# Graph layer kernel: the first six edge tiles of a phase are turned in two groups of three instead of three groups of two

## Chip, cores and metric

The kernel runs on one core of a Trainium2 chip. The metric is the device time of one execution in microseconds (us). Lower is better.

## What is computed

A normalised input goes through three graph layers and is added to the input. 10000 nodes have 512 features; 5000 edges lead from `src` to `dst`.

```
h = relu(layernorm(x))
for layer 0, 1, 2:
    p   = relu(h @ Wp.T + bp)
    agg = segment_sum(p[src], dst) / max(count(dst), 1)
    h   = agg @ Wl.T + bl + h @ Wr.T
    if layer < 2: h = layernorm(relu(h)) * g + be
out = x + h
```

## The kernel before

The three layers are three phases (`l` = 0, 1, 2). A phase has a node part and an edge part. The node part works on tiles of 128 nodes; 71 of the 79 tiles get their product with `Wr` there (`node_product`), the other 8 are "late" tiles, turned at the end of the edge part. The edge part works on 40 tiles of 125 edges, in 10 groups of 4: the normalised rows of the source nodes are gathered, turned, projected with `Wp`, summed along sorted edges, multiplied with `Wl` and added to the rows of the destination nodes.

Every product is made of three fp32r products (low with high, high with low, high with high), so that each operand exists as a high and a low part. To be an operand, a tile must be turned: four 128x128 transposes on TensorE write one PSUM bank (`turn`, L746). ScalarE copies the bank to the high part (`node_xt_high`, L933; `edge_xt_high`, L982), VectorE subtracts that from the bank to get the low part (`xt_low_of`, L1067 in phase 0, L1070 later) and counts `xt_low_done`. Turns use banks 0 and 1 alternately, through all turns of the program, and turn `c` waits until the low part of turn `c - 2` is made.

The order on each engine is written out by hand as one loop over steps `i` of the node part. Step `i` on TensorE holds the turn of node tile `i + 2`, the product of node tile `i` (L758 to L760, 12 matmuls), and whatever else is placed there; the last step with a product is 70. `edge_turns(l, i)` tells every engine which edge tiles are turned in step `i`: TensorE turns them behind the product, ScalarE and VectorE copy and subtract at the end of their step. VectorE's `node_out` of step `i` moves the sum of product `i - 1` out of PSUM. Tiles 6 and 7 are turned behind the first of four projections of group 0 (`project(l, 0, 0)`, L827 to L829, 12 matmuls each). That projection waits for the low parts of tiles 0 to 3. The third projection waits until VectorE has read the first one (`h_pre_of`, L1285). `h_pre`, a scan, `h_high` and `h_low` follow for each projection.

Edge rows are gathered by GpSimd (L610), eight slots deep: once all normalised rows are stored, gathers 0 to 7 are issued, and gather `t` from 8 on waits for the turn of tile `t - 8`. TensorE waits for a tile's gather before it turns it.

Of the kernel before, what the change touches and what calls it, by code (L numbers as in the profile page):

```python
# [25 lines left out]
GROUP = 4  # L26
# [7 lines left out]
AHEAD_XN = 5  # L34
AHEAD_TURN = 2
LATER = (10, 20)
EDGE_TURNS_AT = 3
LATE = 8
LATE_AT = 4
LATE_OUT_AT = (-8, -6, -4, -2, 0)  # L40
# [29 lines left out]
def sage_kernel(nc, x_in, src_cols, dst_cols, dst_rows, weights, out):  # L70
# [20 lines left out]
    with ExitStack() as ctx:  # L91
# [209 lines left out]
        product_count = [NODE_TILES - c for c in late_count]  # L301
# [71 lines left out]
        def is_product(l, n):  # L373
            return 0 <= n < product_count[l]
# [30 lines left out]
        def node_steps(l):  # L405
            return range(-AHEAD_RELU, product_count[l] + 1)

        def edge_turns(l, i):

            first = 2 * (i - (product_count[l] - EDGE_TURNS_AT))  # L410
            return range(first, first + 2) if 0 <= first < 2 * EDGE_TURNS_AT else []

        def edge_turns_beside(s):

# [5 lines left out]
        def late_turns(l, s):  # L420

            first = LATE_TURNS * (s - (EDGE_TILES - GROUP))
            return range(first, first + LATE_TURNS) if first >= 0 and late_count[l] else []
# [307 lines left out]
        def _(pe):  # L731
            def keep_busy(count):

                for _ in range(count):
                    nc.tensor.matmul(bank[7][:, 0:P], ones[:], ones[:], start=True, stop=True)
# [13 lines left out]
            def node_turn(l, t):  # L749
                u = unit_of[l][t]  # L750
                pe.wait_ge(n_xn, l * NODE_TILES + u + 1)
                turn(xn[:, u % XN_RING, :], node_no(l, t))
# [11 lines left out]
            def node_product(l, t):  # L764
                n = products_until(l) + t
                pe.wait_ge(xt_low_done, node_no(l, t) + 1)
                if t >= 4:
                    pe.wait_ge(n_out, n - 3)
                elif l:
                    pe.wait_ge(late_out_done, LATE * l - 3 + t)  # L770
                r_product(l, node_xt(True, t), node_xt(False, t), bank[4 + t % 4][:], n_product)
# [5 lines left out]
            def late_product(l, j):  # L777
                pe.wait_ge(xt_low_done, late_no_of(l, j) + 1)
                if j >= 4 and l == LAYERS - 1:

                    pe.wait_ge(xt_low_done, late_no_of(l, LATE - 1) + 1)
                    pe.wait_ge(e_h_pre, EDGE_TILES * LAYERS)
                elif j >= 4:
                    pe.wait_ge(late_out_done, LATE * l + j - 3)
                else:
                    pe.wait_ge(e_out, EDGE_TILES * (l + 1) - 3 + j)
                r_product(l, late_xt(True, j), late_xt(False, j), bank[late_bank(l, j)][:], late_product_done)

            def count(t):
                pe.wait_ge(hot_done, t + 1)  # L790
                nc.tensor.matmul(bank[2][:, 0:P], hot[:, t % HOT_RING, 0, :], hot[:, t % HOT_RING, 1, :],  # L791
                                 start=(t == 0), stop=(t == EDGE_TILES - 1)).then_inc(counted, 1)

            def turn_carry():
                pe.wait_ge(continues_done, 1)
                pe.wait_ge(counts_copied, 1)
                nc.tensor.transpose(bank[2][0:EDGE_TILES, 0:EDGE_ROWS], continues[0:EDGE_ROWS, :],
                                    ident[0:EDGE_ROWS, 0:EDGE_ROWS]).then_inc(carry_turned, 1)

            def shift_p(l):  # L800
                pe.wait_ge(shift_parts, parts_until(l, "p"))
                for m in range(K):
                    last = nc.tensor.matmul(bank[2][:, m:m + 1], shift_sum[:, m * P:(m + 1) * P], ones[:, 0:1],
                                            start=True, stop=True)
                last.then_inc(shift_p_product, 1)
# [6 lines left out]
            def edge_turn(l, t):  # L812
                pe.wait_ge(e_gathered[t % IN_RING], edge_dma(l, t, IN_RING))
                turn(rows_in[:, t % IN_RING, :], edge_no_of(l, t))
# [38 lines left out]
            for l in range(LAYERS):  # L853
                for i in node_steps(l):

                    if (l, i) == (0, 0):
                        node_product(l, i)
                    if is_product(l, i + AHEAD_TURN):
                        node_turn(l, i + AHEAD_TURN)
                    if (l, i) == (0, -AHEAD_TURN):  # L860
                        keep_busy(WARM_BETWEEN)
                    if l and 0 <= i + LATE < LATE:
                        late_product(l - 1, i + LATE)
                    if is_product(l, i) and (l, i) != (0, 0):
                        node_product(l, i)
                    if l == 0 and 0 <= i - STEP_COUNT < EDGE_TILES // COUNTS:
                        for q in range(COUNTS):
                            count((i - STEP_COUNT) * COUNTS + q)
                    if l == 0 and i == STEP_SORTED + 1:
                        turn_carry()  # L870
                    if l and i == STEP_SHIFT_P:
                        shift_p(l)
                    for t in edge_turns(l, i):
                        edge_turn(l, t)

                for m in range(GROUP):
                    project(l, 0, m)
                    if m == 0:
                        for t in range(2 * EDGE_TURNS_AT, 2 * GROUP):
                            edge_turn(l, t)  # L880
                for s in range(EDGE_TILES):
                    g, i = s // GROUP, s % GROUP
                    for t in edge_turns_beside(s):
                        edge_turn(l, t)
                    for j in late_turns(l, s):
                        late_turn(l, j)
                    if g + 1 < GROUPS:
                        project(l, g + 1, i)
                    edge_product(l, s)
                if l + 1 < LAYERS:  # L890
                    shift_z(l + 1)
# [4 lines left out]
        def _(act):  # L896
# [111 lines left out]
            for l in range(LAYERS):  # L1008
                for i in node_steps(l):
                    for u in units_at(l, i + AHEAD_STD):  # L1010
                        node_std(l, u)

                    if (l, i) == (0, 0):
                        for u in units_at(l, i + AHEAD_XN):
                            node_norm(l, u)
                    if is_product(l, i + AHEAD_TURN):
                        node_xt_high(l, i + AHEAD_TURN)
                    if l:
                        for u in units_at(l, i + AHEAD_RELU):
                            node_relu(l, u)  # L1020
                    if (l, i) != (0, 0):
                        for u in units_at(l, i + AHEAD_XN):
                            node_norm(l, u)
                    for k in R_CHUNKS.get(i, ()) if l == 0 else ():
                        high_r(0, k)
                    if 0 <= i - STEP_SPLIT_P < K:
                        high_p(l, i - STEP_SPLIT_P)
                    if 0 <= i - STEP_SPLIT_L < K:
                        high_l(l, i - STEP_SPLIT_L)
                    for t in edge_turns(l, i):  # L1030
                        edge_xt_high(l, t)
                    for u in units_at(l, i + AHEAD_XN):
                        store_xn(l, u)

                for t in range(2 * EDGE_TURNS_AT, 2 * GROUP):
                    edge_xt_high(l, t)
                for m in range(GROUP):
                    h_high_of(l, 0, m)
                for s in range(EDGE_TILES):
                    g, i = s // GROUP, s % GROUP  # L1040
                    if s >= 1:
                        edge_out(l, s - 1)
                    for t in edge_turns_beside(s):
                        edge_xt_high(l, t)
                    for j in late_turns(l, s):
                        late_xt_high(l, j)
                    if g + 1 < GROUPS:
                        h_high_of(l, g + 1, i)
                    if l + 1 < LAYERS and 0 <= s - STEP_SPLIT_R < K:
                        high_r(l + 1, s - STEP_SPLIT_R)  # L1050
                edge_out(l, EDGE_TILES - 1)

        @block.vector
        def _(dve):
# [248 lines left out]
            for l in range(LAYERS):  # L1303
# [44 lines left out]


                h_pre_of(l, 0, 0)  # L1350
                for t in range(2 * EDGE_TURNS_AT, 2 * GROUP):
                    edge_xt_low(l, t)
                h_sum_of(l, 0, 0)
                for m in range(1, GROUP):
# [6 lines left out]
                for s in range(EDGE_TILES):  # L1361
                    g, i = s // GROUP, s % GROUP
# [60 lines left out]
```

## Time and profile before

| | |
|---|---|
| median of 3 runs | 1511.41 us (1511.03 to 1511.58) |
| the profiled execution | 1511.98 us |
| its span, first to last instruction | 1510.2 us |
| mean granted TensorE clock | 0.999 |
| TensorE matmul busy | 1499.4 us, 99% of the span |
| VectorE busy | 969.7 us, 64% |
| ScalarE busy | 684.0 us, 45% |
| GpSimd busy | 603.7 us, 40% |

In the profile PE is TensorE's matmuls and PEld its weight loads, DVE is VectorE, ACT is ScalarE, POOL is GpSimd and SP is SyncE. A row of the timeline has the start in us, the duration in us, engine, line, operation, destination and sources, shapes, the number of merged instructions, and, in brackets, how long the engine stood idle ahead of it and what ended that. Ends of matmuls are modelled; their starts tell more.

### The profile page before, as it was taken

The numbers are of one execution on the slowest core, as the hardware profiler recorded it, in microseconds if no ns is written. First come the engines' busy times: TensorE is split into PE (matmuls) and PEld (weight loads), VectorE is DVE, ScalarE is ACT, GpSimd is POOL, SyncE is SP. The second block draws the span as 40 slices with busy tenths as digits, with TensorE's granted clock in tenths as the row PEclk, the third lists the DMA queues.
The fourth block names the chain that finished last, engine by engine and source line by source line (L and its number), as shares of the span: only waits on it lengthen the run. The fifth ranks groups of instructions, "written<-read, shape, count | busy, mean of one in ns | idle before, by whom it ended". The sixth has DMA issues, their size and how long they took to land.

```text
span 1510.2 us, 21142 instructions
## 1 busy us (share of the span) xinstructions
PE 1499.4 (99%) x7265; PEld 1224.3 (81%) x7265; DVE 969.7 (64%) x2084; ACT 684.0 (45%) x1267; POOL 603.7 (40%) x532
## 2 busy tenths in 40 slices
PE   9999999999999999999999999999999999999999
PEld 7788888888888888888888888888888877888887
DVE  7999766556555686776565555568767746555552
ACT  5546552322323676776232232357677732232221
POOL 4764355666523000100444432334464463444221
PEclk9999999999999999999999999999999999999999
DMA  9999875555544888786654555489999984554535
GB/s 325 333 358 299 278 258 175 115 91 90 92 84 58 265 272 303 265 287 237 195 112 84 93 89 91 54 255 345 385 354 371 378 257 86 91 89 86 95 58 146
DMA packets 157734, 298.14 MB, mean 197 GB/s; under 512 B 21565, under 2 KB 21756, under 8 KB 157500
## 3 DMA queue, kind: packets, MB, share of 16 engines
q1 hardware_dynamic: 93180, 169.02, 32.6%
q0 software_dynamic: 29744, 64.57, 24.8%
q10 hardware_dynamic: 34704, 63.19, 11.4%
q8 instruction: 59, 0.97, 0.3%
q14 instruction: 47, 0.39, 0.1%
HBM read 136.54 MB, written 160.08 MB: 196 GB/s over the span
## 4 chain that ended last, share of the span: by engine, by line
PE 97%; DMA 1%; issue 1%; SPq 0%; DVE 0%; POOL 0%; ACT 0%
PE bank L758 14%; PE bank L760 14%; PE bank L759 14%; PE bank L746 10%; PE bank L850 7%; PE bank L848 7%; PE bank L849 7%; PE bank L828 7%; PE bank L827 7%; PE bank L829 7%; DMA rows_in<-x 0%; DMA residual<-x 0%; DMA rows_in<-node_x,sorted_src 0%; PE bank L791 0%; PE bank L810 0%
## 5 line engine op out<-in xcount | busy, mean ns | idle before, releaser
L758 PE MATMUL bank<-w_high,h_low 128*128 128x512 f32 x876 | 365.2, 417 | 0.0
L759 PE MATMUL bank<-w_low,h_high 128*128 128x512 f32 x876 | 346.1, 395 | 0.0
L760 PE MATMUL bank<-w_high,h_high 128*128 128x512 f32 x876 | 345.3, 394 | 0.0
L992 ACT ACTIVATE h_high<-h_pre 128x500 fp32r<-128x500 f32 x120 | 74.7, 622 | 450.0 <-DVE h_pre L1294 448.0
L610 POOL DMA_INDIRECT rows_in<-node_x,sorted_src x120 | 123.2, 1027 | 249.8 <-PE bank L746 173.8
L760 PEld LDWEIGHTS bank<-w_high,h_high 128*128 128x128 f32 x876 | 165.5, 189 | 39.9
L827 PE MATMUL bank<-xt_low,w_high 128*128 128x500 f32 x480 | 195.8, 408 | 1.8 <-issue 1.8
L848 PE MATMUL bank<-w_high,h_low 128*125 128x512 f32 x480 | 190.7, 397 | 0.0
L850 PE MATMUL bank<-w_high,h_high 128*125 128x512 f32 x480 | 190.0, 396 | 0.0
L759 PEld LDWEIGHTS bank<-w_low,h_high 128*128 128x128 f32 x876 | 165.4, 189 | 29.6
L849 PE MATMUL bank<-w_low,h_high 128*125 128x512 f32 x480 | 189.3, 394 | 0.0
L758 PEld LDWEIGHTS bank<-w_high,h_low 128*128 128x128 f32 x876 | 165.0, 188 | 29.5 <-DVE h_low L1067 0.2
L637 POOL DMA_INDIRECT node_z<-rows_out,into_i x80 | 128.8, 1610 | 149.6 <-ACT rows_out L1005 118.2
L967 ACT ACTIVATE xn<-rows_in,off,rstd 128x512 f32<-128x512 f32 x237 | 188.0, 804 | 0.0
L828 PE MATMUL bank<-xt_high,w_high 128*128 128x500 f32 x480 | 187.7, 391 | 0.0
L1285 DVE TENSOR_SCALAR h_pre<-bank,bias_p 128x500 f32<-128x500 f32 x120 | 88.6, 738 | 154.2 <-PE bank L829 153.5
L829 PE MATMUL bank<-xt_high,w_low 128*128 128x500 f32 x480 | 187.1, 390 | 0.0
L1070 DVE TENSOR_TENSOR h_low<-bank,h_high 128x512 fp32r<-128x512 f32 x146 | 100.7, 691 | 132.9 <-ACT h_high L933 126.4
L933 ACT ACTIVATE h_high<-bank 128x512 fp32r<-128x512 f32 x213 | 125.5, 589 | 92.5 <-PE bank L746 81.8
L1105 DVE BATCH_NORM_STATS2 stats<-rows_in 128x6 f32<-128x512 f32 x237 | 159.9, 683 | 8.8 <-DMA rows_in<-x 8.8
L628 POOL TENSOR_TENSOR residual<-residual,bias_z 128x512 f32<-128x512 f32 x79 | 102.2, 1295 | 114.6 <-DMA residual<-x 114.5
L1294 DVE TENSOR_TENSOR_SCAN h_pre<-carry,h_pre 128x500 f32<-128x500 bf16 x120 | 143.9, 1200 | 3.8
(116 smaller groups left out, 2265.4 us busy)
## 6 DMA issues: line engine op xcount, KB each, us to landing
node_x<-xn ACTq DMA_DIRECT2D x237, 256.0 KB
rows_in<-node_z SPq DMA_DIRECT2D x158, 256.0 KB
node_z<-rows_out SPq DMA_DIRECT2D x142, 256.0 KB
out<-rows_out SPq DMA_DIRECT2D x79, 256.0 KB, 3.8
rows_in<-x SPq DMA_DIRECT2D x78, 256.0 KB
residual<-x SPq DMA_DIRECT2D x78, 256.0 KB, 5.3
rows_in<-node_x SPq DMA_DIRECT2D x24, 256.0 KB, 2.6
node_z<-bias_z SPq DMA_DIRECT2D x16, 256.0 KB
```

What stands on the lines that cost most here:

```text
L746: last = nc.tensor.transpose(bank[c % 2][:, k * P:(k + 1) * P], rows[:, k * P:(k + 1) * P], ident[:])
L758: nc.tensor.matmul(psum, low[:, k, :], w_high("r", l)[:, k, :], start=(k == 0), stop=False)
L759: nc.tensor.matmul(psum, high[:, k, :], w_low("r", l)[:, k, :], start=False, stop=False)
L760: last = nc.tensor.matmul(psum, high[:, k, :], w_high("r", l)[:, k, :], start=False, stop=(k == K - 1))
L827: nc.tensor.matmul(psum, w_high("p", l)[:, k, cols], low[:, k, :], start=(k == 0), stop=False)
L828: nc.tensor.matmul(psum, w_high("p", l)[:, k, cols], high[:, k, :], start=False, stop=False)
L829: last = nc.tensor.matmul(psum, w_low("p", l)[:, k, cols], high[:, k, :], start=False, stop=(k == K - 1))
L848: nc.tensor.matmul(psum, low, w_high("l", l)[:, m, :], start=(m == 0), stop=False)
L849: nc.tensor.matmul(psum, high, w_low("l", l)[:, m, :], start=False, stop=False)
L850: last = nc.tensor.matmul(psum, high, w_high("l", l)[:, m, :], start=False, stop=(m == K - 1))
L967: S.activation(xn[:, to, :], rows_in[:, slot, :], ACT.Identity, bias=off[:, slot:slot + 1], scale=rstd[:, slot:slot + 1]).then_inc(n_xn, 1)
L1105: V.bn_stats(stats[:, slot, :], rows_in[:, slot, :]).then_inc(n_stats, 1)
```

## The change

The six edge tiles that are turned in the node part are turned in two steps, three in each, where they were turned in three steps, two in each. Before: tiles 0 and 1 in step 68, 2 and 3 in step 69, 4 and 5 in step 70. After: tiles 0, 1 and 2 in step 69, and 3, 4 and 5 in step 70. The loops over the last two tiles of the first two groups (tiles 6 and 7) are written with the new constant and have the same bounds as before.

```
-EDGE_TURNS_AT = 3
+EDGE_TURNS_AT = 2
+EDGE_TURNS = 3
...
         def edge_turns(l, i):

-            first = 2 * (i - (product_count[l] - EDGE_TURNS_AT))
-            return range(first, first + 2) if 0 <= first < 2 * EDGE_TURNS_AT else []
+            first = EDGE_TURNS * (i - (product_count[l] - EDGE_TURNS_AT))
+            return range(first, first + EDGE_TURNS) if 0 <= first < EDGE_TURNS * EDGE_TURNS_AT else []
...
                     if m == 0:
-                        for t in range(2 * EDGE_TURNS_AT, 2 * GROUP):
+                        for t in range(EDGE_TURNS * EDGE_TURNS_AT, 2 * GROUP):
                             edge_turn(l, t)
...
-                for t in range(2 * EDGE_TURNS_AT, 2 * GROUP):
+                for t in range(EDGE_TURNS * EDGE_TURNS_AT, 2 * GROUP):
                     edge_xt_high(l, t)
...
-                for t in range(2 * EDGE_TURNS_AT, 2 * GROUP):
+                for t in range(EDGE_TURNS * EDGE_TURNS_AT, 2 * GROUP):
                     edge_xt_low(l, t)
```

## Rows read from the trace of the kernel before

**Rows 1.** The page: busy time of each engine, and the chain by engine.

```profile
PE 1499.4 (99%) x7265; PEld 1224.3 (81%) x7265; DVE 969.7 (64%) x2084; ACT 684.0 (45%) x1267; POOL 603.7 (40%) x532
...
PE 97%; DMA 1%; issue 1%; SPq 0%; DVE 0%; POOL 0%; ACT 0%
```

**Rows 2.** What TensorE waited for in the run: total us, times, longest.

```profile
PE bank L746 <- issue: 2.3, 3, 1.0
PE bank L827 <- issue: 1.8, 1, 1.8
...
PE bank L746 <- DMA rows_in<-node_x,sorted_src: 0.6, 1, 0.6
```

**Rows 3.** The timeline of phase 0, end of the node part, all engines.

```profile
235.16 0.48 PE L758 MATMUL bank<-w_high,h_low 128*128 128x512 f32 x1
...
237.34 0.40 PE L758 MATMUL bank<-w_high,h_low 128*128 128x512 f32 x1
...
238.04 1.03 PE L746 MATMUL bank<-ident,rows_in 128*128 128x128 f32 x8
...
238.82 0.95 POOL L610 DMA_INDIRECT rows_in<-node_x,sorted_src  x1 [0.30 <-issue]
...
241.39 1.07 ACT L982 ACTIVATE xt_high<-bank 128x500 fp32r<-128x500 f32 x2 [5.35 <-remote]
...
241.62 0.95 POOL L610 DMA_INDIRECT rows_in<-node_x,sorted_src  x1 [1.85 <-remote]
242.01 1.27 DVE L1067 SCALAR_TENSOR_TENSOR xt_low<-bank,xt_high 128x500 fp32r<-128x500 f32 x2 [4.65 <-issue]
...
242.84 1.21 PE L746 MATMUL bank<-ident,rows_in 128*128 128x128 f32 x8 [0.96 <-issue]
...
243.81 0.48 PE L758 MATMUL bank<-w_high,h_low 128*128 128x512 f32 x1
...
246.69 1.03 PE L746 MATMUL bank<-ident,rows_in 128*128 128x128 f32 x8
...
247.48 0.47 PE L827 MATMUL bank<-xt_low,w_high 128*128 128x500 f32 x1
```

**Rows 4.** The timeline of TensorE at the same place of phase 1.

```profile
734.86 1.03 PE L746 MATMUL bank<-ident,rows_in 128*128 128x128 f32 x8
...
739.64 1.22 PE L746 MATMUL bank<-ident,rows_in 128*128 128x128 f32 x8 [0.95 <-issue]
...
744.28 0.47 PE L827 MATMUL bank<-xt_low,w_high 128*128 128x500 f32 x1
```

**Rows 5.** Timelines of phase 2, one engine after the other.

```profile
1231.68 0.60 PE L746 MATMUL bank<-ident,rows_in 128*128 128x128 f32 x4
1232.64 0.66 PE L746 MATMUL bank<-ident,rows_in 128*128 128x128 f32 x4 [0.36 <-issue]
...
1240.77 0.66 PE L746 MATMUL bank<-ident,rows_in 128*128 128x128 f32 x4 [0.57 <-DMA rows_in<-node_x,sorted_src]
1241.18 0.47 PE L827 MATMUL bank<-xt_low,w_high 128*128 128x500 f32 x1
...
1249.62 0.49 PE L827 MATMUL bank<-xt_low,w_high 128*128 128x500 f32 x1 [1.83 <-issue]
...
1232.31 0.59 ACT L982 ACTIVATE xt_high<-bank 128x500 fp32r<-128x500 f32 x1 [2.63 <-issue]
...
1241.69 0.59 ACT L982 ACTIVATE xt_high<-bank 128x500 fp32r<-128x500 f32 x1 [0.86 <-PE bank L746]
1248.88 1.07 ACT L982 ACTIVATE xt_high<-bank 128x500 fp32r<-128x500 f32 x2 [6.60 <-remote]
...
1248.82 0.74 DVE L1285 TENSOR_SCALAR h_pre<-bank,bias_p 128x500 f32<-128x500 f32 x1 [5.24 <-PE bank L829]
...
1244.55 0.95 POOL L610 DMA_INDIRECT rows_in<-node_x,sorted_src  x1 [0.30 <-issue]
1245.80 0.94 POOL L610 DMA_INDIRECT rows_in<-node_x,sorted_src  x1 [0.30 <-issue]
```

**Rows 6.** Busy us by engine in one stretch of phase 2, granted clock, DMA share, GB/s.

```profile
1249.60:1262.00 12.40, 12.38 (x51) 9.99 (x52) 11.99 (x16) 3.79 (x7) 3.72 (x4) 0.86 0.30 81
```

## Prediction

> **What bounds the kernel now.** I read the page's busy times and its chain first. TensorE is busy for 1499.4 of 1510.2 us and 97% of the chain that ended last is TensorE [rows 1], so an edit moves the time by what it does to TensorE's order and pauses. The waits by engine come next: in the whole run TensorE waits some 7 us, of which the largest items are three pauses ahead of turns (2.3 us), one ahead of a projection (1.8 us) and one on a gather (0.6 us) [rows 2]. All three items lie at the end of the node part of a phase, where the change is made, so I read the timeline there.
>
> Phase 0 [rows 3]. The reader should follow one chain. The pair of turns of edge tiles 0 and 1 starts at 238.04. The copy of tile 0 on ScalarE starts only at 241.39, the low part on VectorE at 242.01, and the turn of tile 2, which wants the bank that tile 0 held, at 242.84. TensorE stood for 0.96 us by the row. Product 70 starts at 243.81 and the projection at 247.48. The late link is the first one: ScalarE saw the signal of a turn whose records end near 238.5 only at 241.4, and GpSimd, which waits for the same signal before the gather of tile 8, went on at 241.62. Until 239.8 GpSimd issued gathers back to back. Phase 1 repeats this: turns at 734.86 and 739.64, with 0.95 us idle [rows 4].
>
> Phase 2 differs [rows 5]. ScalarE's copy of tile 0 follows its turn (1231.68) at 1232.31, so signals are on time; tile 1's turn waited 0.36 us and tile 5's 0.57 us for its gather. The signals of the first projection and of turns 6 and 7 then come late: VectorE's h_pre starts at 1248.82 and ScalarE's copy of tile 6 at 1248.88, though the projection ran from 1241.18 to about 1244. The last gather ahead of that started at 1245.80. TensorE idles 1.83 us, and the granted clock is 0.86 in the stretch behind it [rows 6].
>
> **The change, part by part.** Nothing is added: the same 72 transposes, copies and subtractions of six tiles in each of three phases. What moves is the order: tiles 0 and 1 go from behind product 68 to behind product 69, tile 2 stays there as a third, tile 3 goes behind product 70 as the first of three. No DMA is issued by a turn; the gathers of tiles 0 to 7 do not wait for turns, those of tiles 8 to 13 wait for turns 0 to 5. They come later by at most one product and are not wanted before tile 8 is turned beside the first edge product. The edits to the loops of the last two tiles keep their bounds (six and eight) and cost nothing.
>
> The prices, from rows:
> - A pair of turns ahead of the next matmul takes 247.48 - 246.69 = 0.79 us; the eight transposes of rows 3 make 0.44 us a turn, so a last turn costs 0.35.
> - A product behind a turn takes 246.69 - 243.81 = 2.88 us. Its first matmul lasts 0.48 there and 0.40 elsewhere [rows 3], so a product behind a product takes 2.80.
> - From a turn's start to ScalarE's copy of it, when signals are on time: 1232.31 - 1231.68 = 0.63 us [rows 5]. From that copy to the turn that waits for the bank: 242.84 - 241.39 = 1.45 us [rows 3]. Together 2.08.
>
> Without waits, three turns, two products take 2.80 + 1.23 + 2.88 + 1.23 = 8.14 us; the present order, three pairs and two products, 0.79 x 3 + 2.88 x 2 = 8.13. So the move itself is worth nothing, and only the pauses count. There are two banks, and turn c waits until the low part of turn c - 2 is made. In pairs each turn finds a bank that was emptied behind a product. In a group of three the third wants the bank of the first, started only two turns ago. That wait has no cover, since product 70 stands behind turn 2 and the projection behind turn 5: 2.08 - 0.88 = 1.20 us each time.
>
> Phase 0 from 238.04, where product 69 now begins: 2.80 + 2.08 + 0.35 + 2.88 + 2.08 + 0.35 = 10.54, so the projection starts at 248.58 and not at 247.48: +1.10 us. The present pause of about 1.2 us is inside that difference: turn 0's signal is now due near 241.5, when the held-back ones arrived anyway, so it isn't late a second time. Phase 1 from 734.86: 745.40 against 744.28, +1.12. Behind the projection TensorE has the path and nothing gives this back. So 2.2 us from these two; the bounds are 1.6 (0.3 less each, a turn-to-copy link as short as the matmul records allow) and 5.0 (turn 0's signal late again by 1.4 us each, half of what the rows show).
>
> Phase 2 from 1231.68: the projection starts at 1242.22, +1.04. It ends at 1245.0, turns 6 and 7 and the second projection fill up to 1248.7, and the third projection starts at 1249.62 as now, if h_pre is still released at 1248.82: the idle 1.83 us shrinks and takes the delay. That is the lower value, 0. But turn 5 is now due to signal at about 1242.5, between a signal that came in time (ScalarE at 1241.69) and those that came at 1248.8. If it is held until the gathers stop, turn 7, which wants its bank, waits: gather 13 wants turn 5, so the last gather is the one at 1244.55, one step ahead of 1245.80, and the release is near 1247.5. Turn 7 then starts near 1248.9 and the third projection near 1252.1: +2.5 us. I take 0.8, nearer the lower end because ScalarE's copy at 1241.69 is the nearer row. A release 1.25 us earlier bounds it below at -1.25.
>
> Sum: 1.10 + 1.12 + 0.8 = 3.0 us, on the profiled execution 1511.98 -> 1515.0, on the median of 1511.41 (0.04% less) 1514.4. The 0.2% that a measurement of this kernel can tell from no change is 3.02 us, so the forecast lies on that line.
>
> The link that the forecast does not explain is why signals are late. The Trainium skill, "Perfetto Trace Analysis", the section on the Tensor Engine instruction, says that a matmul's recorded end is an estimate and that the semaphore is pushed only when PSUM has acknowledged the writes; the trace agrees, in that records end near 238.5 and the receivers go on at 241.4. By the rule alone the same lag could meet any turn, which is rival E; by the rows it ends with the run of gathers.
>
> **Rivals.**
> A. Turn 5's signal in phase 2 is held until the gathers stop. For: the projection's signal, 1.6 us further on, is held in the trace; the gathers run on without a pause. Against: GpSimd itself needs turn 5. 2.2 + 2.5 = +4.7, so 1516.1. Chance 0.18.
> B. The clock. Rows: in phases 0 and 1 the pause of 1.2 us leaves the granted clock at its 2.4 GHz level, in phase 2 there are 3.4 us at the 1.2 GHz level behind 1.83 us of idling (0.14 x 12.4 = 1.7 us lost) [rows 6]. If two pauses in 6 us bring that drop in phases 0 and 1 too, 2 x 1.7 more: +6.4, 1517.8. The Trainium skill, "TensorE: Matmul & The Clock Gate", Part 1, says the half rate is the default and that activity lifts it, which speaks against every added pause; the trace agrees in phase 2 alone. Chance of this rival: 0.04.
> C. Not slower: in phase 2 turn 5's late signal stops GpSimd one gather early and the held-back projection signal comes 1.25 us sooner, while turn 7 itself isn't held. VectorE's work on the first group, which fills 11.99 of the 12.40 us behind 1249.6 [rows 6], starts earlier. It decides if the release comes at least 1 us before 1248.8. 2.2 - 1.25 = +0.95, 1512.4. Chance 0.15.
> D. The change does not do what the chain says: the present pause goes away because turns now meet idle receivers, and the second pause is covered by records that overstate the chain. About 0, 1511.4. Against it: the wait on the bank is in the code, and 1.45 of the 2.08 us are two operations one behind the other. Chance 0.10, of which 0.04 ends faster.
> E. The lag of turn 0's signal comes back in phases 0 and 1, 1.4 us each, since the signal of product 69 and those of three turns now fall together. For: 2.7 us of such lag in rows 3 and 4. Against: GpSimd stands still from 239.8 until that very signal. 3.0 + 2.8 = +5.8, 1517.2. Chance 0.05.
> Forecast (phase 2 loses 0 to 1.6 us; +2.2 to +3.8, so 1513.6 to 1515.2): 0.48.
>
> **From cases to numbers.** Half of the forecast case is over 3.02 us; with A, B and E that makes 0.51 slower. The other half, C and 0.06 of D make 0.45 same, and 0.04 is faster. The range leaves out B, D and E, 0.19 in all: 1512.2 to 1517.0. The forecast case's own range is 1513.6 to 1515.2.
>
> **What the profile after should show.** TensorE idle ahead of turn 2 and ahead of turn 5 in each phase, 1.2 us each; ScalarE's copy of tile 0 in phases 0 and 1 within 0.8 us of its turn; from product 69's start to the projection 10.5 us. In phase 2 either an unchanged start of h_pre near 1248.8 plus the 2.2 us from before, or a wait of some 3 us ahead of turn 7. Wrong would be: copies of tile 0 that still come 2 to 3 us late (then +2.8 more), no pause ahead of turn 5, or slices of clock under 0.9 in phases 0 and 1.

## The result: 0.2% slower, and the profile after

The changed kernel takes 1514.49 us (median of 16 runs, 1513.6 to 1517.83); the kernel before takes 1511.57 us beside it (16 runs, 1511.03 to 1512.42). The ratio is 1.002, with a 95% interval of 1.0013 to 1.0027: slower by 2.9 us. The profiled execution took 1513.90 us with a span of 1512.1 us. Lines behind the new constant are one higher than before: L746 is L747, L982 is L983, L827 is L828.

What TensorE waited for in the run (total us, times, longest), to be held beside [rows 2]:

```profile
PE bank L747 <- DVE xt_low L1071: 3.2, 3, 1.1
PE bank L747 <- DVE xt_low L1068: 2.2, 2, 1.1
...
PE bank L747 <- issue: 1.1, 1, 1.1
...
PE bank L828 <- issue: 0.7, 1, 0.7
```

Five of the six pauses ahead of turns now carry the name of what ends them, VectorE's low part; the sixth is put down to "issue". Six pauses of 1.05 to 1.15 us have taken the place of three. The timeline of phase 0, all engines, answers to [rows 3]:

```profile
238.62 0.96 POOL L611 DMA_INDIRECT rows_in<-node_x,sorted_src  x1 [0.30 <-issue]
239.80 0.69 DVE L1136 TENSOR_TENSOR rows_out<-bank,bias_z 128x512 f32<-128x512 f32 x1 [2.65 <-remote]
...
240.63 1.03 PE L747 MATMUL bank<-ident,rows_in 128*128 128x128 f32 x8
...
241.36 1.07 ACT L983 ACTIVATE xt_high<-bank 128x500 fp32r<-128x500 f32 x2 [5.53 <-PE bank L747]
...
242.81 0.63 PE L747 MATMUL bank<-ident,rows_in 128*128 128x128 f32 x4 [1.15 <-DVE xt_low L1068]
...
246.06 1.03 PE L747 MATMUL bank<-ident,rows_in 128*128 128x128 f32 x8
246.70 1.07 ACT L983 ACTIVATE xt_high<-bank 128x500 fp32r<-128x500 f32 x2 [2.64 <-PE bank L747]
...
248.15 0.63 PE L747 MATMUL bank<-ident,rows_in 128*128 128x128 f32 x4 [1.05 <-DVE xt_low L1068]
...
248.53 0.47 PE L828 MATMUL bank<-xt_low,w_high 128*128 128x500 f32 x1
```

Turns 0 and 1 stand at 240.63, turn 2 alone at 242.81 behind a pause of 1.15 us; turns 3 and 4 at 246.06, turn 5 at 248.15 behind 1.05 us. ScalarE's copy of tile 0 comes 0.73 us behind its turn; before it came 3.35 us behind. The signal of product 68 is still late: its 12 matmuls end near 238, VectorE goes on at 239.80, just behind the last of the eight gathers. That is 1.97 us behind the start of product 69, where the same step of phase 2 has 0.20 us. The late signals are still there, but turn 0 is no longer held for long.

Phase 1, TensorE alone, answers to [rows 4] and is the same picture:

```profile
740.85 0.63 PE L747 MATMUL bank<-ident,rows_in 128*128 128x128 f32 x4 [1.10 <-DVE xt_low L1071]
...
746.18 0.63 PE L747 MATMUL bank<-ident,rows_in 128*128 128x128 f32 x4 [1.05 <-DVE xt_low L1071]
746.57 0.47 PE L828 MATMUL bank<-xt_low,w_high 128*128 128x500 f32 x1
```

Phase 2, one engine after the other, answers to [rows 5]:

```profile
1238.88 0.63 PE L747 MATMUL bank<-ident,rows_in 128*128 128x128 f32 x4 [1.05 <-issue]
...
1244.22 0.63 PE L747 MATMUL bank<-ident,rows_in 128*128 128x128 f32 x4 [1.05 <-DVE xt_low L1071]
1244.60 0.47 PE L828 MATMUL bank<-xt_low,w_high 128*128 128x500 f32 x1
...
1251.90 0.49 PE L828 MATMUL bank<-xt_low,w_high 128*128 128x500 f32 x1 [0.69 <-issue]
...
1245.39 0.59 ACT L983 ACTIVATE xt_high<-bank 128x500 fp32r<-128x500 f32 x1 [1.55 <-PE bank L747]
1251.17 1.07 ACT L983 ACTIVATE xt_high<-bank 128x500 fp32r<-128x500 f32 x2 [5.19 <-remote]
...
1251.11 0.74 DVE L1286 TENSOR_SCALAR h_pre<-bank,bias_p 128x500 f32<-128x500 f32 x1 [3.83 <-remote]
...
1248.13 0.95 POOL L611 DMA_INDIRECT rows_in<-node_x,sorted_src  x1 [0.30 <-issue]
```

Both pauses are there too. But h_pre of the first projection is released at 1251.11, 2.03 us behind the end of the last gather in front of it (1248.13 + 0.95), nearly as before (1245.80 + 0.94 to 1248.82: 2.08). Counted from the start of product 68 (1228.80 before, 1231.12 after) the release is 20.0 us on in both kernels. So the later first projection only shortens the idle time ahead of the third, from 1.83 to 0.69 us.

The run is best taken apart by one stretch in each phase, from the first matmul of product 68 to the first matmul of the first edge product (us, differences of two starts, taken before rounding, so that the rows can give 0.01 more or less):

| kernel, profiled execution | phase 0 | phase 1 | phase 2 |
|---|---|---|---|
| before | 27.70 | 27.69 | 31.61 |
| before, profiled again (e9) | 27.76 | 27.74 | 31.26 |
| changed | 28.96 | 28.98 | 31.28 |
| changed, profiled again (e10) | 29.09 | 28.97 | 31.46 |

From an edge part's first product to the next phase's product 68 it is 469.1 us in all four (469.33 in one place), and 249.7 to 249.8 us from the last phase's first edge product to the end. So 1.3 us come from phase 0, 1.3 from phase 1, and between -0.3 and +0.2 from phase 2. The first pair of profiled executions differ by 1.9 us: 2.2 from the stretches, less 0.2 at the start and 0.1 at the end. The medians differ by 2.9, since the profiled execution of before lies 0.4 us above its median and that of the change 0.6 below.

### The profile page after: what moved, and what is told of

Read it like the earlier page. It is cut to its first block, busy times and chain, and to the rows that moved or that the text cites. A ratio compares the mean times of both kernels' runs of the same rounds, so it can differ in the third digit from the quotient of the medians.

```text
span 1512.1 us, 21142 instructions
## 1 busy us (share of the span) xinstructions
PE 1498.1 (99%) x7265; PEld 1223.1 (81%) x7265; DVE 970.5 (64%) x2084; ACT 685.1 (45%) x1267; POOL 604.7 (40%) x532
## 4 chain that ended last, share of the span: by engine, by line
PE 96%; DVE 1%; issue 1%; DMA 0%; ACT 0%; another core or an unknown queue 0%; SPq 0%; DVEq 0%
PE bank L759 14%; PE bank L761 14%; PE bank L760 14%; PE bank L747 10%; PE bank L851 7%; PE bank L849 7%; PE bank L850 7%; PE bank L829 7%; PE bank L828 7%; PE bank L830 7%; DMA rows_in<-x 0%; DVE xt_low L1071 0%; DVE h_pre L1295 0%; DVE rows_out L1133 0%
## 5 line engine op out<-in xcount | busy, mean ns | idle before, releaser
L828 PE MATMUL bank<-xt_low,w_high 128*128 128x500 f32 x480 | 195.2, 407 | 0.7 <-issue 0.7
```

Source lines behind the costliest of these rows:

```text
L828: nc.tensor.matmul(psum, w_high("p", l)[:, k, cols], low[:, k, :], start=(k == 0), stop=False)
```

## Experiments

Each was timed against the kernel before on the same chip. In the short diffs the counts are tiles turned in the last steps of the node part: before is (2, 2, 2) in steps 68, 69 and 70, the change is (3, 3) in steps 69 and 70. The last column gives the same stretches as above. "Paced" is explained with e5; e9 and e10 are the two kernels unchanged.

| run | median us | kernel before beside it | ratio, 95% interval | phase 0, 1, 2 |
|---|---|---|---|---|
| e1 (2, 1, 3) | 1513.28 | 1511.47 | 1.0011 (1.0002 to 1.0020) | 28.79, 28.65, 31.30 |
| e2 (3, 3, 0) | 1521.02 | 1511.47 | 1.0063 (1.0049 to 1.0077) | 31.54, 32.33, 31.99 |
| e3 (3, 3), third bank | 1510.66 | 1511.47 | 0.9995 (0.9986 to 1.0004) | 27.20, 27.19, 31.09 |
| e4 (4, 2), four banks | 1509.33 | 1511.47 | 0.9985 (0.9976 to 0.9994) | 26.45, 26.45, 30.92 |
| e9 before again | 1512.36 | 1511.61 | 1.0005 (0.9996 to 1.0014) | 27.76, 27.74, 31.26 |
| e10 changed again | 1514.50 | 1511.61 | 1.0020 (1.0011 to 1.0029) | 29.09, 28.97, 31.46 |
| e5 before, paced | 1505.51 | 1505.65 | 1.0000 (0.9991 to 1.0009) | 26.44, 26.44, 27.63 |
| e6 changed, paced | 1512.47 | 1505.65 | 1.0045 (1.0031 to 1.0059) | 28.91, 28.92, 28.86 |
| e7 (4, 2), paced | 1505.51 | 1505.65 | 1.0001 (0.9992 to 1.0010) | 26.45, 26.45, 27.48 |
| e8 (4, 2), paced by six | 1505.41 | 1505.65 | 1.0000 (0.9991 to 1.0009) | 26.45, 26.45, 27.89 |
| e11 before, paced, again | 1505.11 | 1505.65 | 0.9997 (0.9988 to 1.0006) | 26.44, 26.43, 27.87 |
| e12 changed, paced, again | 1512.23 | 1505.65 | 1.0044 (1.0030 to 1.0058) | 28.87, 28.92, 28.87 |

### One group of three alone (e1), and groups of three one step earlier (e2)

```
-            first = 2 * (i - (product_count[l] - EDGE_TURNS_AT))
-            return range(first, first + 2) if 0 <= first < 2 * EDGE_TURNS_AT else []
+            n = i - (product_count[l] - len(EDGE_TURNS))
+            return range(sum(EDGE_TURNS[:n]), sum(EDGE_TURNS[:n + 1])) if 0 <= n < len(EDGE_TURNS) else []
...
+EDGE_TURNS = (2, 1, 3)    # e1
+EDGE_TURNS = (3, 3, 0)    # e2
```

> Edit of the kernel before: two tiles turned in step 68, one in step 69, three in step 70, so that tiles 0 to 2 are turned no later than before and one group of three is left. Theory (the third turn of a group waits for the bank of the first, 1.2 us, uncovered): no pause of its own in step 69, a pause of 1.05 to 1.2 us ahead of turn 5 in each phase; from product 68 to the first edge product 28.8 us in phases 0 and 1 against 27.7 before; whole run +1.5 to +3.3 us. Rival (it costs because turns, and with them the gathers of tiles 8 on, come a step later): tiles 0 to 2 are not later, so 0 to +0.5 us.

> Edit of the kernel before: groups of three in steps 68 and 69, none in step 70, one step ahead of the change. Theory with signals held while gathers run back to back: the first turn's signal arrives near 241.4 in phase 0 as before, now with nothing to cover it, so turn 2 starts at 242.8 after a pause of some 3.9 us, and a second pause of 1.1 us follows ahead of turn 5; product 70 covers the last low parts; +4.0 us in each of phases 0 and 1, +7 to +10 in all. Rival (a pure bank wait of 1.2 us, the late signal of the trace being of no consequence): two pauses of 1.2 us against one, about +1.1 us a phase, +2 to +3.5 in all.

e1, timeline of TensorE, phase 0:

```profile
242.28 0.63 PE L746 MATMUL bank<-ident,rows_in 128*128 128x128 f32 x4 [0.91 <-issue]
...
247.62 0.63 PE L746 MATMUL bank<-ident,rows_in 128*128 128x128 f32 x4 [1.05 <-DVE xt_low L1067]
```

The old pause ahead of turn 2 is still there (0.91 us) and a new one of 1.05 us stands ahead of turn 5, with tiles 0 to 2 no later than before. A single group of three costs 1.0 to 1.1 us a phase in phases 0 and 1, and +1.8 us in all. So a cost comes without the later place of tiles 0 and 1. In phase 2 the expectation missed the cause: the pause ahead of turn 5 is 1.26 us there and ends with its gather, not with a low part.

e2, timeline of TensorE, phase 0:

```profile
238.12 1.03 PE L746 MATMUL bank<-ident,rows_in 128*128 128x128 f32 x8
242.87 0.63 PE L746 MATMUL bank<-ident,rows_in 128*128 128x128 f32 x4 [3.71 <-DVE xt_low L1067]
...
248.20 0.63 PE L746 MATMUL bank<-ident,rows_in 128*128 128x128 f32 x4 [1.05 <-DVE xt_low L1067]
```

Here turn 2 follows turns 0 and 1 with no product between, at the place where the signals are late. The pause is 3.71 us (3.9 expected), the stretch 3.8 us longer than before, the run +9.5 us. So the signals of [rows 3] do reach the other engines late, and a product of 2.88 us hides most of that in the kernel before. The third turn of the same group waits 1.1 us where signals are on time and 3.7 us where they aren't.

### A bank for each turn of a group (e3, e4)

```
-                last = nc.tensor.transpose(bank[c % 2][:, ...
+                last = nc.tensor.transpose(bank[b][:, ...
...
+            return {2: 2, 5: 3}.get(t, edge_no_of(l, t) % 2)    # e3, with (3, 3)
+            return {2: 2, 3: 3}.get(t, edge_no_of(l, t) % 2)    # e4, with (4, 2)
```

ScalarE's copy and VectorE's subtraction read the same bank, and a turn into bank 2 or 3, which the projections use only later, doesn't wait for `xt_low_done`.

> Edit of the changed kernel: the same groups of three in steps 69 and 70, but the third turn of each goes to a bank of its own (tile 2 to bank 2, tile 5 to bank 3, which the projections use only later). Theory (bank wait): the pause ahead of turn 2 goes, the one ahead of turn 5 goes too, and the first projection then waits some 0.85 us for the low part of tile 3; per phase 1.6 us under the changed kernel and 0.45 us under the one before in phases 0 and 1; whole run -3 us against the change, -1 us against before (-0.5 to -1.5). Rival (later turns or gathers cost): stays at +2 to +3 us over before.

> Tiles 0 to 3 turned in step 69 in four different banks, tiles 4 and 5 in step 70. Theory: no turn waits for a bank and the projection finds the low part of tile 3 made; the late signals of turn 0 are covered by product 70; product 69 to first projection is 8.15 us without a pause, 1.3 us less than before in phases 0 and 1; phase 2 -0.5 to +0.5; whole run -2.6 us against before (-3.5 to -1.5). Rival (what delays signals is not a matter of banks and follows wherever the turns stand): a pause remains, 0 to +1 us against before.

e3 and then e4, timelines of TensorE, phase 0 (the turn is L751, the product L763, the projection L832):

```profile
241.24 1.47 PE L751 MATMUL bank<-ident,rows_in 128*128 128x128 f32 x12
242.47 0.48 PE L763 MATMUL bank<-w_high,h_low 128*128 128x512 f32 x1
...
245.35 1.47 PE L751 MATMUL bank<-ident,rows_in 128*128 128x128 f32 x12
...
247.35 0.50 PE L832 MATMUL bank<-xt_low,w_high 128*128 128x500 f32 x1 [0.52 <-issue]
```

```profile
240.80 1.91 PE L751 MATMUL bank<-ident,rows_in 128*128 128x128 f32 x16
242.46 0.48 PE L763 MATMUL bank<-w_high,h_low 128*128 128x512 f32 x1
...
245.34 1.03 PE L751 MATMUL bank<-ident,rows_in 128*128 128x128 f32 x8
246.13 0.48 PE L832 MATMUL bank<-xt_low,w_high 128*128 128x500 f32 x1
```

In e3 twelve transposes follow one another (x12, no idle time), twice; nothing else than the bank differs from the change, and 1.8 us of the stretch (28.96 to 27.20) are gone in phases 0 and 1. What is left is the projection's wait for tile 3, 0.52 us (0.85 expected). e3's median is 0.8 us under the kernel before, which its interval doesn't tell from no change; against the changed kernel it is 3.8 us less. In e4 the projection finds tile 3 made, the stretch is 26.45 us, the run is 0.15% faster than before (2.1 us, 2.6 expected). Both pauses of the change were therefore waits on a bank.

### Gathers held apart (e5 to e8, e11, e12), and the two kernels again (e9, e10)

```
-                if t >= IN_RING:
-                    pool.wait_ge(turned, edge_no_of(l, t - IN_RING) + 1)
+                behind = 5 if t < 14 else IN_RING    # e8: 6 and 15
+                if t >= behind:
+                    pool.wait_ge(turned, edge_no_of(l, t - behind) + 1)
```

> The kernel before with one edit: gathers 5 to 13 of a phase wait for the turn five tiles back (before: from gather 8 on, eight tiles back), so that no run of eight or more gathers stands back to back ahead of the turns' signals. Theory (signals of TensorE are held while a long run of gathers goes out): ScalarE's copy of tile 0 follows its turn within 0.8 us in phases 0 and 1 and the pause ahead of turn 2 goes; product 68 to first edge product 26.4 us against 27.7; in phase 2 the release of h_pre at the first projection comes in time, 26.4 to 28 us against 31.6; whole run -4 to -7 us. Rival (the signals are late for a reason that does not go with the gathers): copy of tile 0 still 3.3 us behind its turn, 0 us or slower if gathers now land too late.

> The changed kernel with the same pacing of the gathers. Theory: its pauses are waits on the bank and stay at 1.05 to 1.2 us twice a phase, so phases 0 and 1 stay at 28.9 us; phase 2 loses its held signals and comes to 28.9 us from 31.3; -2.4 us against the changed kernel, +6 us against the paced kernel before: the change costs twice as much when the signals of before are on time. Rival (the pauses of the change are late signals too): phases 0 and 1 fall under 28 us.

> Tiles 0 to 3 in step 69 in four banks, 4 and 5 in step 70, and the pacing. Theory: phases 0 and 1 stay at 26.45 us, where nothing waits; phase 2 falls from 30.9 to 26.5 us; -4.4 us against the unpaced one, 1504.9 us. Rival: phase 2's 4 us are not the gathers' doing, 1509 us.

> As the run before, with gathers six tiles ahead and not five. Theory (the length of the run decides): between the two; if a run of six is short enough it equals the five; phase 2 26.5 to 31 us, whole run 1505 to 1509 us.

The expectation that the paced kernels gain over the one before missed: 1505.5 us, but the kernel before, which isn't paced, took 1505.65 us beside them (27 runs), 6 us less than in the measurements above. So I ran both kernels once more, and then both paced ones.

> The kernel before, unchanged, profiled once more beside the changed one, because its time was 1511.5 us in one measurement and 1505.7 us on another chip. Theory (signals held while gathers go out is a thing of some chips, and explains the 6 us): where the time is near 1505.7 the copy of tile 0 follows its turn within 0.8 us in every phase, product 68 to first edge product takes 26.4, 26.4 and 27.6 us, against 27.7, 27.7 and 31.6; where it is near 1511.5 the rows of the first profile come back. Rival (the 6 us lie elsewhere, in the start or in the edge part): the three stretches are the same at both times.

> The changed kernel, unchanged, beside the one before. Theory: its two pauses of 1.05 to 1.2 us in each phase don't depend on the chip. Where the kernel before takes near 1505.7 us the three stretches are 28.9 us each and the change costs 2.5 + 2.5 + 1.3 = +6.3 us (ratio 1.0042); where it takes near 1511.5 us the change costs +3 us (1.002). Rival (the change's cost is 3 us wherever it runs): 1.002 in both.

> The kernel before with gathers 5 to 13 waiting for the turn five tiles back, measured once more, because the first time it ran where the kernel before took 1505.7 us and had no late signals to lose. Where the kernel before takes near 1511.5 us: theory (a long run of gathers holds the signals of TensorE there) the stretches fall from 27.7, 27.7 and 31.6 us to about 26.4, 26.4 and 27.6, whole run -4 to -6.5 us; rival (the gathers have nothing to do with it) 0 us, copy of tile 0 still 3.3 us behind its turn. Where it takes near 1505.7 us: 0 us.

> The changed kernel with the same pacing beside it. Theory: two bank waits of 1.05 to 1.2 us a phase stay whatever the signals do, so 28.9 us in each of the three stretches; +1 us against the kernel before where that takes near 1511.5 us, and +6 us against the paced kernel before everywhere. Rival (the change's cost comes from late signals): it falls with them, and both paced kernels take the same time.

The two unpaced kernels met a measurement at 1511.61 us and gave the rows of the first profiles back (copy of tile 0 at 241.83 for a turn at 238.43, in e9). The paced ones met one at 1505.65 us again. The expectation of e9 put the two levels down to the chip. The record speaks against that: it has chip 8 both for e5 to e8 (1505.65) and for e9 and e10 (1511.61), and chip 2 for e11 and e12 (1505.65). e11, timeline of phase 0, TensorE, then ScalarE, then GpSimd:

```profile
237.75 1.03 PE L747 MATMUL bank<-ident,rows_in 128*128 128x128 f32 x8
...
241.42 1.03 PE L747 MATMUL bank<-ident,rows_in 128*128 128x128 f32 x8
...
238.38 1.07 ACT L983 ACTIVATE xt_high<-bank 128x500 fp32r<-128x500 f32 x2 [2.63 <-PE bank L747]
...
238.62 0.95 POOL L611 DMA_INDIRECT rows_in<-node_x,sorted_src  x1 [2.92 <-PE bank L747]
```

The copy comes 0.63 us behind the turn, and the next turns have no idle time ahead of them. Whether the pacing did that can't be told: it was never run where the kernel before takes 1511.5 us. What speaks against it is only that the kernel before, unpaced, took as little time beside it. The rows around 105 us, where GpSimd issues a long run of indirect stores that the pacing doesn't touch, don't settle it. The kernel before (first pair of rows: TensorE's turn, ScalarE's copy) has a copy 2.48 us behind its turn there, e11 (second pair) 0.87 us. But e1 (third pair), unpaced and measured beside a kernel before of 1511.47 us, has 0.64 us there, though its copy of tile 0 in phase 0 comes 3.29 us behind the turn (last row, for a turn at 237.53). And in e5, which is paced, copies at this place stand up to 2.38 us behind their turns for another reason: VectorE, whose mean ScalarE wants first, waits 2.25 us for a store of rows_out. So late signals around 105 us and in phase 0 don't go together:

```profile
105.36 0.60 PE L746 MATMUL bank<-ident,xn 128*128 128x128 f32 x4
...
107.84 0.60 ACT L933 ACTIVATE h_high<-bank 128x512 fp32r<-128x512 f32 x1 [1.35 <-remote]
```

```profile
105.07 0.60 PE L747 MATMUL bank<-ident,xn 128*128 128x128 f32 x4
...
105.94 0.58 ACT L934 ACTIVATE h_high<-bank 128x512 fp32r<-128x512 f32 x1
```

```profile
104.85 0.60 PE L746 MATMUL bank<-ident,xn 128*128 128x128 f32 x4
...
105.49 0.60 ACT L933 ACTIVATE h_high<-bank 128x512 fp32r<-128x512 f32 x1 [0.84 <-issue]
...
240.82 1.07 ACT L982 ACTIVATE xt_high<-bank 128x500 fp32r<-128x500 f32 x2 [5.29 <-remote]
```

What the paced runs do settle is the change where no signal is late. e12, timeline of TensorE, phase 0:

```profile
242.53 0.63 PE L747 MATMUL bank<-ident,rows_in 128*128 128x128 f32 x4 [1.05 <-DVE xt_low L1068]
...
247.87 0.63 PE L747 MATMUL bank<-ident,rows_in 128*128 128x128 f32 x4 [1.05 <-DVE xt_low L1068]
```

Both pauses are there at 1.05 us, in all three phases, and the stretch is 28.9 us each time against 26.4, 26.4 and 27.6 to 27.9 (in phase 2 the paced kernels without groups of three wait for gathers: e5 0.97 us ahead of turn 1, e7 0.82 us ahead of turn 3, where 26.5 us were expected). The same edit then costs 7.0 and 7.1 us by the medians (1512.47 - 1505.51, 1512.23 - 1505.11) and not 2.9. The stretches give 6.2 and 5.9 of it (86.69 - 80.51 for e6 against e5, 86.66 - 80.74 for e12 against e11). The last 1 us is not located: the paced changed kernel has five runs each time, 1.6 and 2.0 us apart, and the two profiled executions of e12 and e11 differ by 5.9 us.

## Why the prediction was right, point by point

**The move itself is worth nothing, only pauses count.** Right. Product 69 follows product 68 at once and takes 2.80 us (from 237.83 to 240.63 in phase 0), as the term said; what differs between the kernels is idle time.

**The third turn waits 1.20 us for the bank.** Right in kind, shown by e3, and in size. The rows give 1.05 to 1.15 us because they count from the modelled end of two turns (1.03 us) and the sum from 0.88. The chain from turn to the waiting turn is 2.09 us where signals are on time (246.06 to 248.15), 2.08 in the sum; and where no signal is late two groups add 2.43 to 2.49 us to a stretch in phases 0 and 1 (28.91 - 26.44, 28.92 - 26.44, 28.87 - 26.44, 28.92 - 26.43), 1.2 us each. A turn's remainder ahead of the next matmul is 0.38 us in that place, not 0.35. From product 69 to the projection it was 10.60 to 10.70 us, 10.54 in the sum.

**Phases 0 and 1 give 1.10 and 1.12 us.** They gave 1.26 and 1.29 us. In phase 0, 0.1 us of the difference is turn 0's signal, which came 0.73 and not 0.63 us behind its turn, and the rest is the remainder of two turns. In phase 1 it is the chain to turn 2 (738.71 to 740.85, 2.14 us), the two remainders, and 0.05 us behind the projection.

**The present pause is inside that difference, since turn 0's signal is now due when the held-back ones arrive.** Right: due near 241.3 (240.63 + 0.63), seen at 241.36. e2 shows what it costs if that isn't so. Rival E (the lag comes back) is refuted for these places.

**Phase 2 absorbs the delay at the third projection, with 0.8 us on top.** The absorption is right to 0.1 us, the 0.8 was mis-sized: -0.33 against the first profile, +0.20 for e10 against e9. The first profile of before had lost clock in this stretch [rows 6]; the changed one has the following (busy us by engine, then the clock):

```profile
1252.20:1264.60 12.40, 11.44 (x54) 8.92 (x52) 12.10 (x17) 3.48 (x7) 3.85 (x4) 1.00 0.31 86
```

e9 has a granted clock of 1.00 there too, and 31.26 us. From the release of h_pre to the first edge product it is 11.29 to 11.30 us in e9 and in both profiles of the change, and 11.59 in the first profile of before. So the half clock cost the kernel before some 0.3 us there (0.35 in the stretch, 31.61 - 31.26) and not the 1.7 that the prediction read from [rows 6] and rival B charged. The rows fit VectorE as what sets the pace, busy 12.1 of 12.4 us; that was not tried by itself.

**Rival A, turn 5's signal held.** It was late, but not for long: the copy stands 1.17 us behind its turn, where 0.63 is on time (1244.22 to 1245.39) in the first profile, and GpSimd's gathers went on. In e10 it is the mechanism of rival A in small; timelines of ScalarE (copy of tile 5, its turn at 1244.63) and TensorE (turn 7):

```profile
1247.36 0.59 ACT L983 ACTIVATE xt_high<-bank 128x500 fp32r<-128x500 f32 x1 [2.27 <-remote]
...
1248.82 0.63 PE L747 MATMUL bank<-ident,rows_in 128*128 128x128 f32 x4 [0.40 <-issue]
```

The copy is 2.73 us behind and turn 7 waits 0.40 us, which the idle time ahead of the third projection takes up; the 2.5 us of the rival did not come.

**Rival B**: two pauses of 1.1 us in each phase left the granted clock at its 2.4 GHz level (1.00 in all three phases, in both profiles of the change). In e2 it fell in phase 1 behind a pause of 2.94 us and in phase 2 behind pauses of 0.58 and 1.69 us (0.14 x 12 / 0.5 = 3.4 us at the 1.2 GHz level in each), but not in phase 0 behind 3.71 us:

```profile
235.00:247.00 12.00, 8.29 (x49) 6.84 (x47) 3.83 (x6) 2.50 (x5) 6.67 (x8) 1.00 0.77 237
735.00:747.00 12.00, 9.06 (x42) 7.40 (x41) 3.93 (x6) 2.37 (x4) 7.10 (x8) 0.86 0.77 241
1237.00:1249.00 12.00, 9.72 (x45) 7.67 (x44) 3.92 (x6) 2.37 (x4) 9.57 (x10) 0.86 0.76 213
```

The Trainium skill, "TensorE: Matmul & The Clock Gate", Part 1, has the rate halved for want of activity. The traces agree in that the three falls read here stand behind pauses, but not every pause brings one: 1.83 us ahead of the third projection did in the first profile of before, 1.85 us at the same place of e9 did not. So a single pause of this size doesn't tell whether the clock falls. **Rival C** (an earlier release) and **D** (no effect) did not happen.

**The sum.** 3.0 us were forecast and 2.9 measured. The range was earned, the closeness is luck: phases 0 and 1 are 0.3 us above their terms, phase 2 is 0.6 to 1.1 us below its, and the forecast holds only for a measurement in which the signals of before are late. The stretches account for 2.2 us in the first pair of profiles (1.26 + 1.29 - 0.33) and for 2.8 in the second (1.33 + 1.23 + 0.20). The trace of one execution can't say more: the same program differs by 0.05% between e9's median and that of the kernel before beside it (1512.36, 1511.61).

**What stays open.** Why signals of TensorE are late at these places, in some measurements and not in others, and whether the gathers cause it: they run at the same time, but holding them apart was tried only where the kernel before was fast anyway. The prediction had the lateness from one profile, and where the kernel before takes 1505.65 us it would have been some 3 to 4 us short, an estimate from the paced pairs (5.9 to 7.1 us against 3.0).

## What to carry to other kernels

With two buffers, a third item in a row costs the whole round trip through the engines behind it, less what the first two items take (here 2.1 - 0.9 us). Work in pairs with a long operation between, or give the group as many buffers as it has items. Place the group so that the next long operation covers the last round trip: four turns in four banks and then a product, with two turns behind it, had no pause in the stretches of phases 0 and 1. That gained 2.1 us where late signals made the old order wait (e4), and nothing beside a kernel before of 1505.65 us (e7). And price an edit with and without the late signals of one profile: the cost here was 2.9 us where late signals already made the old order wait, and 6 to 7 us where they didn't.

## What the runs showed of the hardware

The same program took 1511.5 to 1511.6 us in three measurements and 1505.65 us in two, with nothing changed in it; chip 8 stands in the record of both. At the higher time its stretches sum to 87.0 and 86.8 us (first profile, e9), and some signals of TensorE arrive late: turn 0 of phase 0 by 2.7 us (3.35 us from turn to copy, against 0.63), the first projection of phase 2 by 4.6 us (7.64 us from its start to h_pre, against 3.06 in e5). At the lower time it wasn't profiled itself; the paced kernel, which takes the same time beside it, has stretches of 80.5 and 80.7 us and no late signal at these places.

The receivers of late signals go on nearly together. In phase 2 of before VectorE starts at 1248.82, ScalarE at 1248.88 and GpSimd at 1249.12, and in phase 0 ScalarE at 241.39 and GpSimd at 241.62. In phase 2 the release of h_pre came 2.0 to 2.2 us behind the end of the last gather in front of it in all four profiles of the two kernels. The records of TensorE show nothing of the lateness: its matmuls start one behind the other until it has to wait itself.
